# Order of router, keys and norm sums in a fused decoder layer: one add on GpSimd behind a wait, one step moved on ScalarE, one on VectorE

## The reference

```python
x = _layernorm(x + _L0_attn_ref(x, ...))            # a state-space scan (Mamba)
x = _layernorm(x + _L0_xattn_ref(x, ctx, ctx, ...)) # mLSTM with 4 heads of 64
x = _layernorm(x + _L0_ffn_ref(x, ...))             # 8 experts, top 2 of a router
```

## Time and profile before

| | us |
|---|---|
| median of 3 runs | 667.14 (665.72 to 668.47) |
| profiled execution, its own time | 670.12 |
| its span | 668.6 |
| TensorE busy | 587.2 |
| VectorE busy | 456.7 |
| GpSimd busy | 287.2 |
| ScalarE busy | 249.0 |

### The profile page before, as it was taken

One profiled execution on the slowest core, in us unless ns is written; L12 is line 12 of the kernel. 1 busy time (PEld: TensorE's weight loads), 2 busy tenths in 40 slices (PEclk: granted clock), 3 DMA queues, 4 the chain that ended last, 5 costly groups with the idle time before them and its releaser, 6 DMA issues.

```text
span 668.6 us, 13885 instructions
## 1 busy us (share of the span) xinstructions
PE 587.2 (88%) x3498; PEld 458.0 (69%) x3499; DVE 456.7 (68%) x1368; ACT 249.0 (37%) x477; POOL 287.2 (43%) x211
## 2 busy tenths in 40 slices
PE   6999989699699888537898989999999999999980
PEld 2444568588356666435687878888888888888870
DVE  2566487956566777876774766777677767677672
ACT  3555540001666653222421424224242242422262
POOL 7100020002092446646570674818576167572323
PEclk9999999899879969557899999999999999999985
DMA  8999607201300006222258475865858547544562
GB/s 269 327 335 336 196 1 203 51 1 43 147 2 1 33 9 259 81 81 95 65 132 224 98 212 146 224 157 136 223 123 232 103 94 218 146 91 94 113 195 91
DMA packets 75418, 93.42 MB, mean 140 GB/s; under 512 B 15869, under 2 KB 70270, under 8 KB 72560
## 3 DMA queue, kind: packets, MB, share of 16 engines
q1 hardware_dynamic: 63280, 78.28, 40.1%
q0 software_dynamic: 6672, 9.58, 7.3%
q10 hardware_dynamic: 5424, 5.05, 3.1%
HBM read 42.93 MB, written 31.67 MB: 112 GB/s over the span
## 4 chain that ended last, share of the span: by engine, by line
PE 63%; DVE 17%; POOL 6%; ACT 4%; DMA 3%; issue 3%; SPq 1%; another core or an unknown queue 1%; POOLq 0%; ACTq 0%; DVEq 0%
PE bank L2408 24%; PE bank L2420 13%; PE bank L1978 8%; PE bank L2137 4%; DMA xcol<-xcol 2%; POOL experts_w L861 2%; DVE region L1383 2%; DVE region L1381 2%; DVE small L1400 1%; PE bank L2028 1%; PE bank L1987 1%; PE bank L2286 1%; POOL small L780 1%; PE bank L1994 1%; PE bank L2242 1%
## 5 line engine op out<-in xcount | busy, mean ns | idle before, releaser
L2408 PE MATMUL bank<-experts_w,experts_x 128*128 (+1 forms) x864 | 215.2, 399 | 2.9 <-issue 2.9
L2408 PEld LDWEIGHTS bank<-experts_w,experts_x 128*128 128x128 f32 x864 | 157.3, 188 | 36.5 <-issue 3.7
L2420 PEld LDWEIGHTS bank<-experts_w 128*128 128x128 f32 x840 | 106.5, 194 | 6.6 <-issue 3.7
L2420 PE MATMUL bank<-experts_w 128*128 x840 | 107.7, 285 | 3.1 <-DVE region L1867 1.8
L909 POOL DMA_INDIRECT total<-region,rid x32 | 49.5, 1547 | 113.9 <-DVE region L1867 92.0
L1173 ACT ACTIVATE region<-bank 128x512 f32<-128x512 f32 x72 | 42.3, 597 | 129.2 <-PE bank L2408 115.8
L780 POOL TENSOR_TENSOR small<-small 128x4 f32<-128x4 f32 (+5 forms) x21 | 26.4, 1259 | 112.7 <-DVE small L1392 92.1
L1843 DVE TENSOR_TENSOR xcol<-region,bank 128x512 f32<-128x512 f32 x72 | 49.1, 682 | 37.1 <-ACT region L1173 37.0
L1179 ACT CAST experts_w<-bank 128x512 fp32r<-128x512 f32 x70 | 40.5, 587 | 71.7 <-DVE bank L1852 64.6
L1978 PE MATMUL bank<-xcol,region 128*128 128x512 f32 x128 | 58.1, 612 | 7.4 <-DMA xcol<-in_xT 5.8
L889 POOL TENSOR_TENSOR experts_w<-wstage,experts_w 128x2048 f32 x12 | 55.3, 4625 | 12.8 <-ACT experts_w L1197 12.8
(11 more groups left out here) (368 smaller groups left out, 933.8 us busy)
## 6 DMA issues: line engine op xcount, KB each, us to landing
wstage<-in_w_exp SPq DMA_DIRECT2D x18, 1024.0 KB, 5.2
xcol<-xcol SPq DMA_DIRECT2D x140, 128.0 KB
slots<-padrow SPq DMA_DIRECT2D x8, 2210.0 KB, 19.7
wstage<-in_w_exp SPq DMA_DIRECT2D x2, 3072.0 KB, 12.1
region<-slots ACTq DMA_DIRECT2D x34, 130.0 KB
xcol<-in_xT SPq DMA_DIRECT2D x4, 512.0 KB, 6.6
xtok<-in_x SPq DMA_DIRECT2D x1, 2048.0 KB, 13.3
region<-in_ctxT SPq DMA_DIRECT2D x1, 2048.0 KB, 7.6
```

What stands on the lines that cost most here:

```text
L2408: mm = pe.matmul(bank[2 * u + m][:, :], (xTh, xTl)[a][:, s, k, :], moving(off, w, m * KD * F + k * F + u * HALF, HALF), start=(k == 0 and ...
L2420: mm = pe.matmul(bank[into][:, 0:D], (high, low)[a][:, u, c, :], moving(off, w, 2 * KD * F + (4 * u + c) * D, D), start=(u == 0 and c == 0 ...
```

## The change

Three edits. GpSimd multiplies the heads as before, but for u of 1 and 2 waits until VectorE has written the router's arguments u times before it adds them to the residual. ScalarE scales its keys before the router's exponentials. VectorE places the routed rows before it takes the norm sums.

```diff
                 link(pool.tensor_tensor(rows, rows, bc(onw[:, :], 1, [P, n, D]), ALU.mult))
+                if u:
+                    pool.wait_ge(rexp_in, u)
                 pool.tensor_tensor(here, here, rows, ALU.add).then_inc(resid_done, 1)
...
-                if i in RANK_AT:
-                    router_exp(RANK_AT[i])
                 if i in TURN_AT:
                     norm2_turned(TURN_AT[i])
                 if b + 1 < B and c in (1, 2):
                     weigh_keys(b + 1, range(3 * c - 3, 3 * c))
+                if i in RANK_AT:
+                    router_exp(RANK_AT[i])
...
                 if b and c == 2:
-                    norm2_stats(b - 1)
                     if b >= 2:
                         route_place(b - 2)
+                    norm2_stats(b - 1)
```

## The result

| | before | changed |
|---|---|---|
| median, 22 runs each | 667.7 us (664.75 to 669.43) | 665.12 us (663.43 to 670.49) |
| ratio | | 0.9974 (0.9961 to 0.9986) |
| profiled execution, own time | 670.12 us | 666.16 us |

The change makes the kernel faster: by 0.26% by the ratio (1.7 us), by 2.6 us or 0.39% by the two medians. Forecast were 4.2 us (ratio 0.9936, 0.64%): the sign is right and the time lies in the range, but the gain is 0.4 of the forecast by the ratio and 0.6 by the medians. Two later measurements of the same code (experiments 9 and 13) gave 0.9926 (0.9899 to 0.9952) and 0.9963 (0.9934 to 0.9992), so the measured gain differs from one set of runs to the next. What takes most of it, when it is taken, is what follows. Two executions of the experiments took over 1400 us and are left out of the comparisons.

The account below looks back on a forecast made before the run. The edited stretch, 240 to 290 us, was taken as a chain hopping between engines with TensorE partly idle. Gains at both places net 4.2 us at place 2's scatters: profiled 670.12 to 665.9, median 667.14 to 662.9; range 660.4 to 666.0.

Parts of the forecast that it names:

- Edit 1, port: GpSimd's add stalls VectorE instructions reading two SBUF operands; moving it removes 1.83 us at place 1, 2.1 at place 2.
- place 1: Tiles 9 to 11 (norm sums of batch 1, routing of batch 0): GpSimd's L807 of place 2 starts 4.0 us earlier.
- rival 2: Nothing arrives: the moved add also holds VectorE's PSUM-fed instructions, nothing won at place 2's scatters; 667 us, chance 0.11.
- place 2: Tiles 13 to 15 (batch 2, batch 1): router 6.1 us earlier, part handed back, scatters from 272.65, 4.2 us earlier.
- I take the quick pair: Place 1, last batch's states: L2242 takes 1.62 us and the rest 1.84, not 2.87 and 3.14, its gap being gone.
- L807 ends at 261.7 and frees L1616: Start of place 2: GpSimd's multiply ends and releases VectorE's router, which ends at 265.7, 6.1 us earlier.
- GpSimd, not TensorE, now carries the gain: End of place 1: GpSimd's scatters and root set the pace and hand 4.0 us to its L807 of place 2.
- Rival 1: Clock stays low at place 1: L1539 only 2.7 us earlier, place 2's scatters 2.9 us earlier; 664.2 us, chance 0.22.
- Total: 4.2 us won by 284 us, nothing changed behind: 665.9 us for the profiled execution, 662.9 for the median.
- What is won by 284 us reaches the end one for one: Behind 290 us every step waits for the one before, so time won or lost by about 284 us reaches the end.

Follow-up runs that it names:

- 9: The changed kernel measured again with no edit: ratio to before 0.9926 (0.9899 to 0.9952), 666.69 against 670.73 us.
- 13: The changed kernel measured a third time with no new edit: 664.72 us, ratio to before 0.9963 (0.9934 to 0.9992).
- 3: Changed kernel plus ten extra matmuls in TensorE's gap before it turns batch 1's rows: ratio to before 0.9912, median 661.99 us.
- 7: Changed kernel plus ten extra matmuls before turning batch 1's rows and 24 before the last batch's: ratio to before 0.993.
- 8: Changed kernel plus ten extra matmuls before batch 1's turning, with tiles 13 and 14 put back as before: ratio 0.9959, median 663.68 us.
- 11: Changed kernel plus ten extra matmuls before turning batch 1's rows and 38 before the last batch's: ratio to before 0.9915.
- 14: The code of 3 again, beside the unedited changed kernel on one chip: 662.0 us, ratio to before 0.9918.
- 15: Changed kernel with only the ranks' read ahead of the norm sums, plus eight extra matmuls before batch 1's turning: 660.07 us, ratio 0.9895.
- 16: Changed kernel plus four extra matmuls before turning batch 0's rows and ten before batch 1's: 660.2 us, ratio to before 0.9904.
- experiment 5: Changed kernel with the router's exponential put back ahead of the key scalings: ratio to before 0.9959 (0.993 to 0.9988).
- 2: Changed kernel without GpSimd's wait before the residual add, the other two edits kept: ratio to before 1.0003 (0.9981 to 1.0024).
- 4: Kernel before plus eight extra matmuls in its own gap ahead of the last batch's states: ratio 0.9963 (0.9943 to 0.9982).
- 1: Kernel before with only GpSimd's wait added, the add behind the router's arguments: ratio 0.9984 (0.9957 to 1.001).
- 10: Changed kernel with only the ranks' read ahead of the norm sums, rest of placing behind: ratio to before 0.9971, median 669.02 us.
- 12: Kernel before plus ten extra matmuls ahead of turning batch 1's rows, where 1 us was idle: ratio 0.9989 (0.9969 to 1.001).

## Why the prediction was right and wrong

- *Edit 1, port*: right. Stalls of 2.02 and 2.29 us are gone (0.19 us each now). At place 1 L1654 is held to the add's end, and PSUM-fed instructions are not; rival 2 is refuted. At place 2 L1654 was held in the profile of 13 (0.98 us) and not in the profile after (0.25), where it started at 271.77, behind the add's end at 271.61.
- *Place 1*: right in every term: the add, L2244's start and length, sums at 247.44 (forecast 247.95), L1596 at 247.78 (248.3), L807 at 259.18 (259.35). Part of this agreement is luck, since the stage ran 0.2 to 0.9 us ahead before the edited instructions began. "I take the quick pair" came true.
- *The step that failed*: "L807 ends at 261.7 and frees L1616". The sum lets place 2's router start when GpSimd's multiply ends; it has no term for TensorE's matmuls in front of tile 13's sums and so takes them as ready, at full clock, by then. L807 did end at 261.53, but VectorE waited 4.19 us for those matmuls, the sums started at 264.56, and the router's last instruction, L1635, ended at 269.1 instead of 265.7. So the 4.2 us at place 2's scatters were 0.4 us. The gap of TensorE was not gone, it had moved: the sum itself had the values ready at 247.6 and gave the rows to be turned no earlier than 248.3, and I wrote "GpSimd, not TensorE, now carries the gain" without asking what TensorE does meanwhile. It idles 2.6 us, and in two of the three profiles of the changed kernel its clock then halves for some 20 us; in the third it halves for 3.4 us, the sums start at 260.29 and the scatters come 4.9 us earlier than before. The price of the low clock, from two profiles of one code: logits 3.42 - 1.85 us, and the rest in the matmuls around them; together 5.1 us of the stretch (34.9 against 29.8), more than the 4.2 that were forecast.
- *What is shown of the cause*: with the gap filled (3, 7, 8, 11, 14, 15, 16) the clock stayed full at the turning and for more than 5 us behind it in every profile, and the ten extra matmuls alone took 2.7 us off the median on one chip. What decides whether the fall lasts 3 or 20 us stays open. It isn't the length of the gap in front of L2297: 3.4 us of low clock followed gaps of 1.96 and 1.79 us, some 20 us followed 2.63 and 2.62, but 17 us followed a gap of 1.00 us (experiment 5).
- *Rival 1* named the clock, at the wrong place (ahead of L2242's successors) and at a price of 1.3 us instead of 5.1. The sentence there, from the page "TensorE: Matmul & The Clock Gate" of the Trainium skill (Part 1), that the clock turns at other moments from run to run, is now borne out by the traces: 0.50 and 0.88 between 252 and 264 us for one code.
- *Place 2*: right in size where the clock was up. The sum's 30 us became 29.5 (3) and 29.8 (13); in 13 the last router instruction ended at 264.9 (forecast 265.7), then came add, placing, norm sums and root in a row, and the scatters at 271.96 (272.65).
- *Total*: the medians moved by 2.6, 4.0 and 2.8 us in three sets. That fits a mixture of the two outcomes on both sides (the kernel before has its own gap, worth 2.7 us when filled), but the share of each was not measured: a profile shows one execution, and the timed ones have a mean clock for the whole execution and no trace.
- *"What is won by 284 us reaches the end one for one"* can't be read from the profiles of before and after, because of the wait at 306 us, which differs by 3 us. It stays open what that wait is. From the profile after to that of 13, with that wait at 0.82 and 1.54 us, the 4.5 us at place 2's first scatter are 3.2 us at the end, so it holds in the main and not to the last microsecond.

## What to carry to other kernels

An engine that is made faster gets a gap further on, and for TensorE a gap may not be free even off the path: find where it will wait next and what stands behind that, and give the sum a second value with the matmuls there at half clock. Where such a gap can't be closed, matmuls into a bank that is about to be overwritten were a cheap mend here (ten of them: 2.7 us of 665), but not where the work behind the gap was thin (38 of them: nothing more). And compare two profiles by a stretch around the edit, not by their spans, and profile the unchanged code twice: here the spans agreed with the forecast while the edited stretch had gained nothing, and the next profile of the same code looked different.

## What the runs showed of the hardware

- The same program on the same inputs ran 12 us at a granted clock of 0.50 in one execution and 0.88 in another, with a gap of 2.63 against 1.79 us in front. In the first, the clock stayed at 0.50 for some 20 us, in which TensorE counted as busy nearly all the time.
- Matmuls of 8 columns (the logits, 1.85 us) were followed by a fall of the clock within 0.4 us of their end, with TensorE counted as busy, in the profiles of 2, 3, 4, 7, 8, 11, 14 and 15, and not in those of before, 1, 10, 12, 13 and 16. What decides between the two is open.
- GpSimd's `pow` instruction (L780, 128x16, 2.93 us) did not hold up a VectorE instruction with two SBUF inputs, while its add and its multiply did (L1609 2.29 us, L1616 1.18 us at 264.59 beside L807, 0.19 alone): in the kernel before L1573, with two such inputs, started at 259.93 inside the root that runs from 257.72 to 260.65, and took its usual 1.22 us. Another L1573 (128x768) ran from 282.42 to 283.37 wholly inside the root from 281.71 to 284.01.
